# Mixer transform on half-precision pairs, attention begun with one chunk, last head sums of the mixing reordered

## The reference

```python
k = fno_layer(tokens_norm, key_w, ..., (Hs, Ws)); q = ...; v = ...
dprod = softmax(einsum('bhtd,bhsd->bhts', qf, kf) / scale)       # 16 heads
attn = fno_layer(einsum('bhts,bhsd->bhtd', dprod, vf), proj_w, ...)
attn = instance_norm(attn + tokens, ...)
m = instance_norm(attn, ...)
m = fno_layer(m, mixer_w1, ..., norm=..., act=gelu)    # Fourier modes 0..16 and skip
m = fno_layer(m, mixer_w2, ..., norm=...)
out = instance_norm(m, ...) + attn
```

```python
dist2 = |Q|^2 + |K|^2 - 2 Q K^T
t = t + softmax(exp(-dist2)) V          # per batch of 4096 tokens
t = t + top-2 of 8 experts(layer_norm(t))
```

## Time and profile before

| | us |
|---|---|
| median of 3 runs (lowest, highest) | 2350.61 (2346.66, 2353.24) |
| profiled execution | 2354.32, its span 2352.4 |
| TensorE busy | 2082.6 (89%) |
| VectorE busy | 1882.0 (80%) |
| ScalarE busy | 1665.1 (71%) |
| GpSimd busy | 602.9 (26%) |

### The profile page before, as it was taken

One profiled execution on the slowest core, in us unless ns is written; L12 is line 12 of the kernel. 1 busy time (PEld: TensorE's weight loads), 2 busy tenths in 40 slices (PEclk: granted clock), 3 DMA queues, 4 the chain that ended last, 5 costly groups with the idle time before them and its releaser, 6 DMA issues. The chain is left out here.

```text
span 2352.4 us, 30833 instructions
## 1 busy us (share of the span) xinstructions
PE 2082.6 (89%) x10374; PEld 1067.8 (45%) x10374; DVE 1882.0 (80%) x3586; ACT 1665.1 (71%) x2413; POOL 602.9 (26%) x750
## 2 busy tenths in 40 slices
PE   7767859865899999999999999999999999767778
PEld 7722437732444444444444444444444444333333
DVE  4666887688778889889888888889888888867776
ACT  1444236464778888888888888878888888667666
POOL 1035415335302202102102102112000001046668
PEclk9978655555999999999999999999999999889999
DMA  9003560000000000000000000000000000000101
GB/s 301 9 1 143 153 151 3 1 1 6 1 10 1 1 1 1 1 1 1 1 1 1 1 1 1 1 1 1 1 1 1 1 1 1 0 14 28 32 28 46
DMA packets 80833, 55.72 MB, mean 24 GB/s; under 512 B 11283, under 2 KB 78739, under 8 KB 79140
## 3 DMA queue, kind: packets, MB, share of 16 engines
q1 hardware_dynamic: 75476, 52.38, 7.4%
q10 hardware_dynamic: 5200, 1.38, 0.3%
HBM read 36.91 MB, written 16.78 MB: 23 GB/s over the span
## 5 line engine op out<-in xcount | busy, mean ns | idle before, releaser
L2004 ACT ACTIVATE inner<-banks,key_bias,scales 128x1024 f32<-128x1024 f32 x512 | 617.2, 1205 | 212.5 <-PE banks L1821 207.3
L2189 DVE TENSOR_TENSOR weights_low<-weights,weights_high 128x1024 f16<-128x1024 f32 x512 | 674.4, 1317 | 17.0
L2011 ACT ACTIVATE weights<-inner 128x1024 f32<-128x1024 f32 x512 | 541.1, 1057 | 17.3 <-DVE weights_low L2189 1.6
L2185 DVE CAST weights_high<-weights 128x1024 f16<-128x1024 f32 x512 | 371.3, 725 | 175.8 <-ACT weights L2011 161.6
L2295 POOL CAST sums_high<-sums 128x512 f16<-128x512 f32 x32 | 39.1, 1221 | 1089.2 <-ACT sums L1983 1071.3
L1821 PE MATMUL banks<-queries_high,keys_high 128*128 128x512 f16 x1024 | 304.5, 379 | 0.7 <-ACT inner L2004 0.7
L1836 PE MATMUL banks<-weights_high,tokens_low 128*128 128x512 f16 x1024 | 304.6, 379 | 0.0
L1821 PE MATMUL banks<-queries_low,keys_high 128*128 128x512 f16 x1024 | 304.6, 379 | 0.0
L1821 PE MATMUL banks<-queries_high,keys_low 128*128 128x512 f16 x1024 | 304.6, 379 | 0.0
L1836 PE MATMUL banks<-weights_low,tokens_high 128*128 128x512 f16 x1024 | 304.6, 379 | 0.0
L1836 PE MATMUL banks<-weights_high,tokens_high 128*128 128x512 f16 x1024 | 304.5, 379 | 0.0
(11 more groups left out here) (613 smaller groups left out, 3243.0 us busy)
## 6 DMA issues: line engine op xcount, KB each, us to landing
images_b<-in_x SPq DMA_DIRECT2D x32, 256.0 KB, 9.4
images_a<-in_x SPq DMA_DIRECT2D x8, 1024.0 KB, 9.8
mixed_scratch<-images_a SPq DMA_DIRECT2D x4, 2048.0 KB, 13.1
result<-group_result SPq DMA_DIRECT2D x32, 256.0 KB, 2.3
images_b<-mixed_scratch SPq DMA_DIRECT2D x10, 768.0 KB, 5.2
images_a<-in_x SPq DMA_DIRECT2D x10, 768.0 KB, 9.1
mixer_weights<-in_L_conv_mixer_w SPq DMA_DIRECT2D x4, 272.0 KB, 6.8
table<-tables ACTq DMA_DIRECT2D x1, 772.5 KB, 7.1
```

The source lines that it names most:

```text
L2004: act.activation(m.inner[:, t % 2, :], m.pair[t % 2], ACT.Exp, scale=m.fs[:, 1:2], bias=m.kb[:, c // QN % 2, k:k + 1]).then_inc(s.inner, 1)
L2011: act.activation(m.wt[:, t % 2, :], m.inner[:, t % 2, :], ACT.Exp).then_inc(s.outer, 1)
L2185: vec.tensor_copy(m.wH[:, t % DEEP, :], m.wt[:, t % 2, :]).then_inc(s.high, 1)
L2189: vec.tensor_tensor(m.wL[:, t % DEEP, :], m.wt[:, t % 2, :], m.wH[:, t % DEEP, :], ALU.subtract)\
```

## The change

1. Mixing: for the last k, `reduce(k - 1)` is called behind q of 3 instead of 1.
2. First mixer layer: ScalarE evicts the forward transform as half precision (times 8) into `m.half17H`; VectorE makes the rest (`halved`) into `m.half17L`, for set b-3 behind the statistics of set b-1, and the last three at the end. `forward(b)` waits for `s.halved` of set b-2.
3. Mixer: the second transform is two half-precision matmuls a column, the high part against high and low tables (68 moving columns) and the low part against the high table (34), in five rounds. ScalarE evicts the high columns scaled, VectorE adds the others. One sum for the statistics moves behind the last round. ScalarE first does a Sqrt on one column.
4. Attention: ahead of step 0 only chunk 0 is finished, and chunk 1 is transposed; `norm(1, 0)` and `norm(1, 1)` follow behind scores(2), the other two in step 0, `norms(1)` in step 1. ScalarE squares and VectorE sums chunk 1 in steps 0 and 1. `norms(0)` goes ahead of the second query, which now uses the bank of the first. Chunk 1 is prepared on GpSimd alone. ScalarE first does an Exp on one column.

```diff
-                if k and q == 1:
+                if k and q == (1 if k < len(MT) - 1 else 3):
                     reduce(k - 1)
...
                 if b >= 2:
-                    pe.wait_ge(s.copied, b - 1)
+                    pe.wait_ge(s.halved, b - 1)
...
-                act.copy(images(m.half17, b), m.ps[6 + b % 2][:, 0:n * FM].rearrange("p (t x) -> p t x", t=n))\
-                    .then_inc(s.copied, 1)
+                act.activation(images(m.half17H, b), m.ps[6 + b % 2][:, 0:n * FM].rearrange("p (t x) -> p t x", t=n),
+                               ACT.Copy, scale=8.0).then_inc(s.copied, 1)
...
+            def halved(b):
+
+                vec.wait_ge(s.copied, b + 1)
+                n = width(b)
+                y = m.ps[6 + b % 2][:, 0:n * FM].rearrange("p (t x) -> p t x", t=n)
+                vec.scalar_tensor_tensor(out=images(m.half17L, b), in0=y, scalar=8.0, in1=images(m.half17H, b),
+                                         op0=ALU.mult, op1=ALU.subtract).then_inc(s.halved, 1)
...
                     (gelu_statistics if kind == 'mix1' else statistics)(b - 1)
+                if kind == 'mix1' and b >= 3:
+                    halved(b - 3)
...
-    rounds = [(0, 12), (12, 24), (24, 34)]
+    rounds = [(0, 7), (7, 14), (14, 21), (21, 28), (28, 34)]
...
-                    mm = pe.matmul(m.ps[r][:, (xf - lo) * FM:(xf - lo) * FM + FM], m.half17[:, :, xf], m.dft17,
-                                   start=True, stop=True)
+                    at = m.ps[r][:, (xf - lo) * 2 * FM:(xf - lo) * 2 * FM + 2 * FM]
+                    pe.matmul(at, m.half17H[:, :, xf], m.dft17P, start=True, stop=False)
+                    mm = pe.matmul(at[:, 0:FM], m.half17L[:, :, xf], m.dft17P[:, 0], start=False, stop=True)
...
+            act.activation(m.col[:, 31:32], m.unity[:, 0:1], ACT.Sqrt)
+            for r, (lo, hi) in enumerate(rounds):
+                act.wait_ge(s.second, r + 1)
+                act.activation(m.feat[:, lo:hi, :], pieces(r, lo, hi)[:, :, 0], ACT.Copy, scale=2.0 ** -10).then_inc(s.evicted, 1)
...
-                vec.wait_ge(s.second, r + 1)
-                e = vec.tensor_copy(m.feat[:, lo:hi, :].rearrange("p x y -> p (x y)"), m.ps[r][:, 0:(hi - lo) * FM])
+                vec.wait_ge(s.evicted, r + 1)
+                e = vec.scalar_tensor_tensor(out=m.feat[:, lo:hi, :], in0=pieces(r, lo, hi)[:, :, 1], scalar=2.0 ** -10,
+                                             in1=m.feat[:, lo:hi, :], op0=ALU.mult, op1=ALU.add)
...
 def norm_at(n, i):
-    return {2: 6 + i, 3: 14 + i, 4: 24 + i}.get(n, (n - 4) * KT + 18 + 2 * i)
+    return {1: i // 2 - 1, 2: 6 + i, 3: 14 + i, 4: 24 + i}.get(n, (n - 4) * KT + 18 + 2 * i)
...
-            for n in (0, 1):
-                turn(n, 0)
-                turn(n, 1)
-                for i in range(4):
-                    norm(n, i)
-                if n == 0:
-                    query(0, 0)
-                    query(0, 1)
-                norms(n)
+            turn(0, 0)
+            turn(0, 1)
+            for i in range(4):
+                norm(0, i)
+            query(0, 0)
+            norms(0)
+            query(0, 1)
+            turn(1, 0)
+            turn(1, 1)
             for t in range(LEAD):
                 scores(t)
+            norm(1, 0)
+            norm(1, 1)
...
                 act.activation(m.wt[:, t % 2, :], m.inner[:, t % 2, :], ACT.Exp).then_inc(s.outer, 1)
+                if t < 2:
+                    square(1, 2 * t)
+                    square(1, 2 * t + 1)
...
+                if t < 2:
+                    reduce(1, 2 * t)
+                    reduce(1, 2 * t + 1)
```

More of the change, by code:

```diff
@@ L1044, in stage_inverse @@
     s = semaphores(nc, held, "inverse_" + kind, "in0 in1 in2 in3 v sized rooted total scaled turned high low first bhigh "
-                   "blow rows used lin ready saved forward copied weights cleared algebra affine added gstat partly")
+                   "blow rows used lin ready saved forward copied halved weights cleared algebra affine added gstat partly")
     arrived = [s.in0, s.in1, s.in2, s.in3]
@@ L1360, in _ @@
             (gelu_statistics if kind == 'mix1' else statistics)(len(sets) - 1)
+            if kind == 'mix1':
+                for b in range(len(sets) - 3, len(sets)):
+                    halved(b)
 def stage_factors(nc, held, m):
@@ L1452, in stage_mixer @@
 def stage_mixer(nc, held, m):
-    s = semaphores(nc, held, "mixer", "v ones second sums summed added rooted spread rows")
-    rounds = [(0, 12), (12, 24), (24, 34)]
+    s = semaphores(nc, held, "mixer", "v ones second evicted sums summed added rooted spread rows")
+    rounds = [(0, 7), (7, 14), (14, 21), (21, 28), (28, 34)]
     zr, zi, t1, t2 = (m.spare[:, NM * k:NM * k + NM] for k in range(4))
@@ L1748, in side_uses @@
 def side_uses():
-    order = []
-    for n in (0, 1):
-        order += [('turn', n, 0), ('turn', n, 1)] + [('norm', n, i) for i in range(4)]
-        order += [('query', 0, 0), ('query', 0, 1)] if n == 0 else []
-        order.append(('norms', n))
-    placed = [(norm_at(n, i), ('norm', n, i)) for n in range(2, CHUNKS) for i in range(4)]
+    order = [('turn', 0, 0), ('turn', 0, 1)] + [('norm', 0, i) for i in range(4)]
+    order += [('query', 0, 0), ('norms', 0), ('query', 0, 1), ('turn', 1, 0), ('turn', 1, 1)]
+    placed = [(norm_at(n, i), ('norm', n, i)) for n in range(1, CHUNKS) for i in range(4)]
     placed += [(turn_at(n, low), ('turn', n, low)) for n in range(2, CHUNKS) for low in (0, 1)]
-    placed += [(norms_at(n), ('norms', n)) for n in range(2, CHUNKS)]
+    placed += [(norms_at(n), ('norms', n)) for n in range(1, CHUNKS)]
     placed += [(query_at(c, h), ('query', c, h)) for c in range(1, CHUNKS) for h in (0, 1)]
@@ L1933, in _ @@
                 values(t)
-                for n in range(2, CHUNKS):
+                for n in range(1, CHUNKS):
                     for i in range(4):
@@ L1994, in high_next @@
                 act.copy(m.lnH[:, t], banked(m, t % 2)).then_inc(f.high, 1)
-            for n in (0, 1):
-                for i in range(4):
-                    square(n, i)
+            act.activation(m.rden[:, 7:8], m.ident[:, 0:1], ACT.Exp)
+            for i in range(4):
+                square(0, i)
             for t in range(STEPS):
@@ L2297, in split @@
                     pool.tensor_tensor(m.oL[:, part], m.oS[:, part], m.oH[:, part], ALU.subtract).then_inc(s.split, 1)
[L2299 to L2303 removed]
+            for i in range(4):
+                prepare(0, i)
+            pool.wait_ge(s.prepared_v, 1)
+            for n in range(1, QN + 1):
                 for i in range(8):
```

85 lines of the change are left out of this document (40 added, 45 removed).

## The result

| | before | changed |
|---|---|---|
| median of 8 runs each, us | 2350.06 (2346.66 to 2353.24) | 2334.93 (2333.44 to 2343.05) |
| ratio, 95% interval | | 0.9942 (0.9928 to 0.9956) |
| profiled execution, its span, us | 2354.32, 2352.4 | 2333.92, 2331.8 |

The account below looks back on a forecast made before the run. The prediction took TensorE to bound the attention loop, and barriers or engine chains the edited stages; -2.0 + 4.6 - 9.2 - 2.8 = -9.4 us gave a median of 2341.2 us, range 2335.5 to 2349.5.

Parts of the forecast that it names:

- Mixing, -2.0: Mixing: moving the reduction ends the stage on the store's landing instead of VectorE, 2.0 us earlier, not 3.0.
- First layer, +4.6: First mixer layer: added low halves on the VectorE and ScalarE ring cost 4.6 us (3.3 to 6.5).
- the free third position: First mixer layer: the third low half of a period falls into VectorE's 2.09 us wait and costs nothing.
- rival (c): First mixer layer: low halves hidden as linear instructions miss GpSimd's additions; layer +0.5, whole 2337.1 us; chance 0.10.
- TensorE's stall: First mixer layer: transforms waiting for low halves stall TensorE 2.2 and 1.3 us, taken up by slack, priced at nothing.
- Mixer, -9.2: Mixer: the second transform in half precision lets the modes begin 9.2 us earlier (-8.1 to -9.9).
- I take 0.11: 7.5 us: Mixer's second transform: 68 half-precision matmuls at 0.11 us each, from a row of 128-column transposes, take 7.5 us.
- Attention, -2.8: Attention start: first scores 10.9 us earlier, mostly given back to norms and squares; chunk 2's turn 2.8 us earlier.
- (a): Attention start: clock stays at 1.2 GHz in the squares' gaps, +3.5 instead of -2.8, whole 2347.5 us; chance 0.20.
- (b): Attention start: the clock is at the high level from the start, whole 2338.9 us; chance 0.12.
- (d): First mixer layer: TensorE's new waits lie on the path, 2.6 us a period, 26 in all, whole 2367; chance 0.06.
- (e): Mixer: the transform is bound by strided loads and gains half, 4.6 us less, whole 2345.8 us; chance 0.07.

Follow-up runs that it names:

- twice_2: Changed kernel with the low half of each period's third set in the first mixer layer formed twice; first layer 122.5 us, against 122.3.
- three: Changed kernel with each mixer matmul of 68 columns split into two of 34; first matmul to modes 7.8 us instead of 5.8.
- attention_only: Kernel before with only the attention begun with one chunk; ratio to before 0.9996 (0.9984 to 1.0007).
- spread: Changed kernel with chunk 1's four squares spread one each over steps 1 to 4, its norms at step 3; ratio to before 0.9943.
- first_early: Changed kernel, first layer: ScalarE's high half moved earlier, TensorE's first inverse step put ahead of the forward transform; ratio to before 0.9937.
- best: Changed kernel with the first layer's high half moved earlier, chunk 1's squares spread over steps 1 to 4, norms at step 4; ratio to before 0.9890.
- pace_only: Changed kernel with GpSimd's preparation of chunks 3 and 4 held back to steps 4 to 11 and 12 to 19; ratio to before 0.9941.

## Why the prediction was right, and where its size was off

**Mixing, -2.0: right**, with its reason: 23.3 to 21.4 us in both kernels that have the moved reduction, and the store's landing, not VectorE, at the end.

**First layer, +4.6: right in sum (+4.7), by luck.** The place of a low half alone is 0.20 (0.22 said), and the free third position is shown by twice_2. But a period grew by 0.36, not 0.44, and from other terms than mine: two places of 0.20, less 0.34 that the linear instructions gave back, plus 0.20 and 0.11 by way of TensorE. Two steps of mine failed there. I kept the neighbours at their price; rival (c) was largely true: VectorE's linear instructions took 45.3 us in all before and 41.9 in the changed kernel, because the moved ones miss GpSimd's additions (the third of a period, 1.71 us before, takes 1.37). And I priced TensorE's stall at nothing, though my own figures had a transform ending at 404.3 and the gelu wanting its buffer at 404.0. The cover fell short: in each period one gelu came 0.4 and one 0.1 us late. Nine periods grew by 3.1 us in all (4.0 said), the short last one by 1.0 (0.2 said), and the end of the stage by 0.6 (0.4 said). The errors cancelled.

The Trainium skill (VectorE: DVE Perf Modes, TRN2 errata) gave 0.27 us for the low half; its record is 0.27 to 0.28, its place in the stream 0.20. The rule holds for the instruction, the sum needs the spacing.

**Mixer, -9.2: the step that failed.** It is the term "I take 0.11: 7.5 us", which measured 0.06 and 4.0: 3.5 us, and with it -12.7 instead of -9.2, outside my ends of -8.1 and -9.9. The nearest row had the right type, load and clock, but moved 128 columns, and I took its 0.11 for the price of the load. It was the price of the columns: two matmuls of 512 columns at this level take 0.85 us (574.34 to 575.19 above), 0.83 ns a column, and 128 of them 0.106. With 128 columns the columns' own time hides what is fixed. The row to go by was not the one with the same load but one with as few columns, or, where none is, a lower end of nothing more than the columns' own time (34 and 68 columns: 0.03 and 0.06). three shows that what is left is fixed for a matmul. The range of the whole had no place for such a gain in a term, which is why its low end, 2335.5, fell just beside the median of 2334.93. Its high end has a slip as well: it adds +1.5 for the attention, where the end stated is +3.5, which would give 2350.5 instead of 2348.5.

**Attention, -2.8: direction and mechanism right, size half.** First scores -10.6 (said -10.9), two gaps of 2.13 and 2.42 (said 2.0 and 2.1), the first steps at the low level, then 1.00 without a fall. The turn of chunk 2 came 1.6 us earlier and the last scores 1.2, since each step of the chain of scores, inner, norms and squares was some tenths longer. In the other kernels with this code that distance was 36.3 to 37.7 us (38.2 before): its own spread is as large as the gain. attention_only says the same: 0.9996.

**Rivals.** (a) is out: the clock reads 1.00 in the windows of both gaps, of 2.13 and 2.42 us. The length of a gap alone doesn't decide it. In the same trace the level had fallen just ahead of the first scores, around gaps of 2.60 and 1.21 us with short groups between them; in the kernel before it fell between 595 and 597, around gaps of 1.25, 1.30, 0.40 and 1.00 us; and in spread it fell in the one gap of 5.21 us behind a full TensorE. The Trainium skill (TensorE: Matmul & The Clock Gate, HAM oscillation) describes a stream that falls back to the low level in each wait of some 3 to 5 us for a transfer; the gap in spread agrees with it. (b) is out: the first scores ran at 0.50. (d) is out in its size, not in its mechanism: TensorE waited 12.5 us for the low halves in the layer, and through the gelu 0.3 us a period of that reached the period, not 2.6; first_early shows the mechanism at work in full. (e) is out: the strided loads cost nothing that shows.

**The sum.** By the marks: -1.9 (mixing) + 4.7 - 12.7 - 1.2 (attention) = -11.1 us, inside the interval of -10.3 to -16.9; with the 1.2 us that go with the clock between the modes and the statistics it is -12.3. The forecast's -9.4 is just outside the interval. The 1.3 us from -12.3 to the ratio's middle are assigned to nothing; the interval is wider than that.

## What to carry to other kernels

Price an instruction by a row with the same amount of the thing that paces it, and ask of each near row what paced it; the lower end of the range must go below the nearest row when the new instruction is smaller. When work is taken from the head of a loop, see which in-order engine gets it: here the gaps that ScalarE's squares make were the largest part of the 9.0 us given back out of 10.6, and each cure moved the wait to VectorE. When a wait is to be covered by slack, compare it with every buffer that the waiting instruction frees: tenths of a microsecond there were worth as much as the instructions that were added. And look at the wait that is in the kernel before as well: one instruction queued behind five that were less urgent cost 1.1 us a period, 11.4 us in all, nearly as much as the whole change won.

## What the runs showed of the hardware

- At a granted clock of 0.50, matmuls of half precision, each with a load of 128 columns, stand 0.06 us apart with 34 and with 68 moved columns, and 0.107 apart with 128 (the transposes of the earlier trace rows and those behind them).
- VectorE and GpSimd slow each other. VectorE's subtraction of 1024 elements with two inputs in SBUF took 1.94 us beside GpSimd and 1.23 alone; GpSimd's product of 508 took 1.89 beside VectorE's loop and 1.03 before it began:

Timeline of GpSimd in best, before and after VectorE's first low half of the loop (about 575):

```profile
568.16 1.03 POOL L2306 TENSOR_TENSOR centred<-centred,token_factors 128x508 f32<-128x508 f32 x1
...
576.75 1.89 POOL L2306 TENSOR_TENSOR centred<-centred,token_factors 128x508 f32<-128x508 f32 x1
```

The Trainium skill (SBUF — State Buffer, section on the two separate sides) has GpSimd and a VectorE instruction with two inputs in SBUF take one port pair in turn, whole instructions at a time. Both sides growing agrees with it. Here a VectorE cast of 1024 elements with one input grew too: 0.69 us alone, and 1.50 in pace_only beside a product of GpSimd that kept its 1.03.

- The level of the clock changes at different moments in executions of the same code: one stretch took 34.2 us at a mean clock of 0.87 in its last part and 35.9 at 0.62, both in kernels with the change of the mixer. Single differences of a microsecond need the window's clock beside them.
